# Three early load waits taken out of a tiled Gram-matrix kernel

## What is computed

```python
def reference(inputs):                       # (2048, 64, 256) float32
    Z = jnp.einsum('bnd,bmd->bnm', inputs, inputs)
    n = inputs.shape[1]
    li, lj = jnp.tril_indices(n, k=-1)
    return Z[:, li, lj]
```

## Time and profile before

| | |
|---|---|
| median of 3 runs | 437.03 us (436.17 to 438.0) |
| profiled execution, its own time | 437.67 us |
| its span, first to last instruction | 435.9 us |
| TensorE busy (matmuls) | 385.4 us, 88% |
| VectorE busy | 363.7 us, 83% |
| ScalarE busy | 179.3 us, 41% |
| GpSimd busy | 197.2 us, 45% |
| data moved by DMA | 151.01 MB, mean 346 GB/s |
| granted TensorE clock, mean | 0.975 of full |

### The profile page before, as it was taken

How to read it: one execution, slowest core, us unless ns; L and a number is a source line. 1 busy time by engine, 2 the same in 40 slices (tenths; PEclk the granted TensorE clock), 3 DMA queues, 4 the chain that set the end, 5 groups by cost and what they waited for, 6 DMA issues and landing times.

```text
span 435.9 us, 68822 instructions
## 1 busy us (share of the span) xinstructions
PE 385.4 (88%) x33024; PEld 377.5 (87%) x33024; DVE 363.7 (83%) x224; ACT 179.3 (41%) x834; POOL 197.2 (45%) x980
## 2 busy tenths in 40 slices
PE   4569999999999999999998999989899998989810
PEld 4569999999999999999998989989899998989810
DVE  5248899999999999897997979799697979979734
ACT  0101125454444535354444544533445454345372
POOL 0000082745628174471817446281744628173584
PEclk9999999999999999999999999999899999999965
DMA  5589999999999999999999999999999999999416
GB/s 199 192 312 388 387 387 387 387 391 392 387 398 386 402 387 368 369 394 357 356 398 344 390 377 387 353 352 378 373 384 368 379 365 373 361 386 368 107 34 156
DMA packets 72378, 151.01 MB, mean 346 GB/s; under 512 B 4640, under 2 KB 4768, under 8 KB 72352
## 3 DMA queue, kind: packets, MB, share of 16 engines
q1 hardware_dynamic: 72352, 150.75, 95.3%
HBM read 134.22 MB, written 16.52 MB: 346 GB/s over the span
## 4 chain that ended last, share of the span: by engine, by line
PE 35%; DMA 28%; DVE 16%; SPq 10%; issue 6%; POOL 3%; ACT 0%; DVEq 0%; POOLq 0%
PE bank_set L256 35%; DMA x_in<-x_dram 25%; DVE x_turned L203 12%; SPq L138 9%; DVE row_halves L219 3%; DMA y_dram<-packed_rows 3%; POOL packed_rows L122 3%; DVE packed_rows L122 1%; DVE x_turned L225 0%; SPq L145 0%; ACT packed_rows L117 0%; ACT products L282 0%; DVEq L202 0%; DVEq L218 0%; DVEq L64 0%
## 5 line engine op out<-in xcount | busy, mean ns | idle before, releaser
L256 PE MATMUL bank_set<-x_turned 32*64 32x64 f32 x33024 | 385.4, 237 | 30.0 <-issue 12.1
L256 PEld LDWEIGHTS bank_set<-x_turned 32*64 32x64 f32 x33024 | 377.5, 132 | 37.8 <-issue 21.9
L203 DVE STREAM_TRANSPOSE x_turned<-x_in 128x2048 f32<-128x2048 f32 x128 | 290.6, 2286 | 58.0 <-DMA x_in<-x_dram 41.5
L122 POOL COPY packed_rows<-row_halves 32x60 f32<-32x60 f32 (+30 forms) x961 | 194.9, 204 | 232.3 <-DMA y_dram<-packed_rows 132.5
L282 ACT COPY products<-bank_set 128x768 f32<-128x768 f32 (+2 forms) x96 | 69.0, 729 | 215.4 <-PE bank_set L256 204.9
L219 DVE STREAM_TRANSPOSE row_halves<-products 128x1024 f32<-128x1024 f32 x64 | 76.8, 1203 | 6.9 <-POOL packed_rows L122 5.0
L117 ACT COPY packed_rows<-row_halves 128x128 f32<-128x128 f32 x256 | 56.4, 300 | 17.4 <-DMA y_dram<-packed_rows 15.9
L111 ACT COPY packed_rows<-row_halves 128x32 f32<-128x32 f32 (+30 forms) x481 | 62.3, 220 | 0.0
L282 ACT ACT_TABLE_LOAD x1 | 1.3, 1283 | 15.8 <-PE bank_set L256 15.8
L122 DVE COPY packed_rows<-row_halves 32x2 f32<-32x2 f32 (+30 forms) x31 | 3.5, 191 | 0.0
L225 DVE MEMSET x_turned<- 128x2048 f32 x1 | 1.8, 1765 | 1.2 <-PEq L325 1.2
## 6 DMA issues: line engine op xcount, KB each, us to landing
x_in<-x_dram SPq DMA_DIRECT2D x256, 512.0 KB, 10.8
y_dram<-packed_rows SPq DMA_DIRECT2D x30, 504.0 KB, 9.6
y_dram<-packed_rows SPq DMA_DIRECT2D x2, 380.0 KB, 3.9
y_dram<-packed_rows SPq DMA_DIRECT2D x2, 124.0 KB, 3.9
```

The costliest lines, as they stand in the source:

```text
L122: return copy(packed_rows[first:first + BLOCK, group % 2, :, at + BLOCK:at + i], row_halves[first + BLOCK:first + HALF, i, :, 0:i - BLOCK])
L203: nc.vector.transpose(x_turned[:, j].rearrange("p k c (i r) -> p k r c i", r=JOINED), x_in[:, k].rearrange("p k (r c d) -> p k r c d", r=J ...
L256: done = nc.tensor.matmul(bank_sets[s][side * HALF:(side + 1) * HALF, g, at, :], rows, rows, start=c == 0, stop=c == CHUNKS - 1)
```

## The change

The three waits go, and with them the constant that named their tiles. SP then issues the first eight tiles, 16 DMAs, without a wait.

```diff
--- before.py
+++ after.py
@@ -27,8 +27,6 @@
     TILE = SIDES * PER_SIDE
     TILES = BATCHES // TILE
     IN_RING = 8
-
-    APART = range(2, 5)
     ARRAY_TILES = QUADRANTS * SIDES
 
 
@@ -129,9 +127,6 @@
                 if t >= IN_RING:
                     lap, j = place(t - IN_RING)
                     sync.wait_ge(turned[j], (lap + 1) * LAP)
-                elif t in APART:
-
-                    sync.wait_ge(loaded[t - 1], SIDES * 16)
                 group, in_group = divmod(t, GROUP_TILES)
                 for side in range(SIDES):
                     first = (group * GROUP + side * KEPT + in_group * PER_SIDE) * BLOCK
```

## The result

| | before | changed |
|---|---|---|
| median of 15 runs | 437.08 us (436.17 to 438.57) | 439.44 us (438.25 to 440.5) |
| profiled execution, span | 435.9 us | 437.7 us |

The ratio is 1.0051, with a 95% interval of 1.0039 to 1.0063. The change makes the kernel slower by 2.4 us, 0.5%. The forecast of 432.0 has the wrong sign, although the time lies inside the range.

The account below looks back on a forecast made before the run. TensorE sets the pace first, loads later, SP's queue the end. A 5.2 us gain off the profiled 437.67 gives 432.5, off the median 437.03 gives 431.8; forecast 432.0, range 429.5 to 443.5.

Parts of the forecast that it names:

- What bounds the kernel: Whole run: TensorE sets the pace first, loads later; the end hangs on SP's queue, tile 127 turned at 410.13.
- (2): Loads of the first tiles: with the queue never empty, tile 8 lands at 33.5 instead of 39.0, gaining 5.5 us.
- (3): TensorE's first loop pass: four code fetches at 5.10 us each put the last burst at 30.3, 2.5 us later.
- the high bound: TensorE's first pass: a block of code costs at most 5.7 us, last burst at 32.7.
- rival A: TensorE's first pass: a fetch waits for every load queued ahead of it, slower, about 446 us; chance 0.22.
- (4): Up to tile 54: TensorE's 2.5 us delay costs nothing at the end but limits the loads' lead; gain taken 5.2 us.
- tightest place: Tile 30's load, which needs tile 22 turned: 14.05 us from free slot at 85.94 to landing at 99.99.
- the room: At tile 30: what gain and TensorE's delay together may use, 7.4 to 9.4 us.
- (5): After tile 54: loads become late again between 275 and 305 us, then the same queue runs 5.2 us earlier.
- B: TensorE's first pass: no change, fetches under a full queue cost 5.7 us or a little more, 434.5 to 437.5; chance 0.17.

Follow-up runs that it names:

- two tiles in flight: Kernel before, but tiles 2 to 7 are each issued when the tile two ahead has landed: 436.79 us against 436.9, ratio 0.9987.

## Why the prediction was wrong

**What bounds the kernel:** right. Loads bound the late part, and the end hangs on the store that POOL waits for: tile 127 is 1.53 us later, POOL 1.56 us and the span 1.8 us.

**(2), the loads:** right in kind, too small. Tile 8's second half in the changed kernel, issued and landed (us to landing in the last column of the second row):

```profile
15.91 2.54 SPq L133 DMA_DIRECT2D x_in<-x_dram  x1
...
x_in<-x_dram SPq DMA_DIRECT2D x1, 512.0 KB, 12.7
```

It landed at 28.6, 10.4 us earlier, where I had 33.5. From tile 1, turned at 9.33, seven tiles took 19.3 us, hardly more than the 18.9 without any fetch, though three packets of code lay between. I had charged 1.3 us for each on the slowest DMA engine. In this full queue three fetches cost the loads 0.4 us together; it is TensorE that pays.

**(3), TensorE's code:** this step failed. I took 5.10 us a block, "the one with the most loads issued beside it", and called 5.7 the high bound. The four cost 6.20, 6.20, 6.19 and 6.47. The last burst came at 35.51, and from tile 4 on TensorE was 7.7 to 8.1 us late instead of 2.5. What was wrong is the reading of the earlier trace rows: in the kernel before, the waits under study keep the queue short just when a block is asked for. When the block of 5.10 was due, from 22.73 us on, only tile 4 was queued ahead of it (issued at 22.10), and tiles 5 to 7 were only being issued. The first packet, which overtook part of tile 1, showed that a fetch isn't behind *all* loads (rival A, bursts 10 us or more apart, did not come), but not that the queue's depth costs nothing. Of the rule in the Trainium skill, "DMA: Bandwidth & Descriptors", section on queues, rings and completion order, by which a DMA engine takes turns between its queues, the trace bears out that a fetch is not put behind the whole queue: 6.2 us, while a load of that time took 12.7 us to land. But I had concluded from it that depth does not matter, and two tiles in flight against a full queue (4.83 and 5.10 against 6.20) show that it does, at least up to some tiles.

**(4), is the delay on the path:** the mechanism was right, but its tightest place was not tile 30. "Gain and TensorE's delay together may be 7.4 to 9.4 us": with a delay of 8.1 us measured (tile 22 turned at 91.74 instead of 83.67), and 5.8 us instead of 4.7 from a freed buffer to landing, the room is 14.05 - 5.8 = 8.3 us, and leaves 0.2. Tile 30 landed 0.2 us earlier. The same sum for tile 31, behind the first store, says more: its buffer was free at 88.53 and it landed at 105.1, 16.6 us later; in the changed kernel a load just issued needed 9.4 us there (96.62 to 105.98). The room is 7.2 us, less than TensorE's delay of 8.1, and so the tile is 0.9 us late. With 6.2 us a block and nothing else changed the prediction's TensorE would have been 9.9 + 24.8 - 27.83 = 6.9 us late: 0.5 to 2.5 us of gain left by its room at tile 30, 0.3 us by the room at tile 31. The price of a block takes nearly all of the forecast gain; the loss itself needs the rest of the delay too (a first burst 0.6 us later, a last block of 6.47, and 0.4 us within the last burst).

**What no step had:** the first store behind a short queue, which is why tile 31's room is smaller. Tile 31's second half was issued at 97.28 and took 8.7 us to land, 106.0, which is 6.2 us behind tile 30; before it was issued at 92.30 and took 12.8, 105.1, 5.1 us behind tile 30. By bytes, 3.29 MB moved from 95 to 105 us instead of 3.96.

**(5), the rest:** the first wait of VectorE for a load after the start was forecast for 275 to 305 us with about five of them; it came at 290.59, and there are six, 15.1 us in all. The rest followed the queue, now with the other sign.

**The rivals:** B is what happened: its mechanism, with its "four of 6.7 make it 8.9 us late and leave nothing". Its price stopped at 437.5 and would have had to go on to 439.4. I gave it 0.17, and 0.01 of that to slower. The words "or a last burst at 33 or later (B)" were the test, and it came out so.

## What to carry to other kernels

A wait that leaves DMA engines idle at the start may be paying for something that isn't in the kernel's text: here the first pass of a long TensorE loop, whose code comes by the same engines. Before such a wait is taken out, price what shares the engines with a *full* queue, and not from rows in which the wait keeps it short. A lead of loads is only worth what the ring can hold: compare (room between a buffer's release and its landing) with (gain plus the consumer's delay) at the tightest tile. Pacing the loads, so that at most one and a half tiles are under way, kept TensorE's code on time and most of the loads: some 3 us faster than no wait at all, and not to be told from the waits that were there (436.09 against 436.9 us).

## What the runs showed of the hardware

That the bursts wait for code is read from the trace: each of the five waits ends 2.2 to 2.9 us after a packet of 16 KB on the queue of kind instruction has started, in every profile of this case, and in the whole run that queue moves six. A block of 128 matmuls and 128 weight loads cost TensorE 3.45 to 4.0 us from burst to burst with no load under way, 3.5 to 5.9 with up to two tiles queued, and with more queued mostly 6.2 to 7.0 (6.2 three times in a row within 0.01 us), once 7.8.

The same program doesn't always take the same first pass. In the kernel before with only its stores moved, whose first 90 us have the same instructions, the profiled execution had these bursts:

```profile
15.53 2.36 PE L256 MATMUL bank_set<-x_turned 32*64 32x64 f32 x128 [3.29 <-issue]
20.36 2.37 PE L256 MATMUL bank_set<-x_turned 32*64 32x64 f32 x128 [2.47 <-issue]
28.20 2.26 PE L256 MATMUL bank_set<-x_turned 32*64 32x64 f32 x128 [5.47 <-issue]
34.40 5.83 PE L256 MATMUL bank_set<-x_turned 32*64 32x64 f32 x377 [3.94 <-issue]
```

Its last block came 6.6 us later than in the profile of the kernel before, while its tile 4 had landed 4.9 us earlier (23.2 instead of 28.1). The kernel before with 7 buffers shows the same (last block at 33.86). So a single profile of the first 30 us, which the prediction was built on, is one of several that this kernel can have, and the 7.7 us between the last blocks of the two profiles compared above is not all the change's doing. By the rule of 402.2 us a last block at 34.4 would end a kernel before at 436.6 us, an estimate; that is 0.7 us above the profiled 435.9 and 1.1 us below the changed kernel. How often the kernel before takes which pass, and why, is not known. All five profiles without any load wait had their last block at 34.1 to 37.4 us.

The stretch with the first store ran slower where the store met a short queue: 325 GB/s against 399 in the stretch above. Why, was not tried.
